# Another order of the same steps in a 16-batch block of attention and experts

## The chip, the cores and the metric

The kernel runs on one core of a Trainium2 chip. A core has five engines that run side by side, each with its own queue of instructions: the matrix engine (TensorE, PE in the profile), VectorE (DVE), ScalarE (ACT), GpSimd (POOL) and SyncE (SP), which here only issues transfers. They tell each other of finished work by semaphores. The metric is the device time of one execution in microseconds; a version's time is the median of its runs.

## What is computed

For 16 batches of 256 rows of 256 numbers the reference computes three things one after the other. First a block with attention, whose layer norms are shifted and scaled by a condition vector:

```python
ada = t_emb @ w_ada + b_ada
sh_msa, sc_msa, g_msa, sh_mlp, sc_mlp, g_mlp = jnp.split(ada, 6, axis=-1)
xn = layer_norm(logmap0(x))
xm = expmap0(xn * (1 + sc_msa) + sh_msa)
q = _to_heads(plin(xm, w_q, b_q))
attn = jax.nn.softmax(scores, axis=-1)
x = mobius_add(residual, expmap0(attn_t))
...
ff = plin(plin(xm, w_f1, b_f1), w_f2, b_f2)
return mobius_add(residual, expmap0(ff_t))
```

Then, on its result, attention over a window of 64 rows with 16 heads, joined by a gate with attention over 64 latents with 8 heads, and added to x:

```python
local = _local_window_attn(Q, K, V)
rem = jnp.einsum('bhsn,bhnd->bhsd', lp, GV)
out = gl * local + gr * rem
return out @ w_out
```

Last a feed-forward network with four low-rank experts, of which two are weighed in for each row, on a modulated copy of x, and added to x again:

```python
base = jnp.einsum('bsd,fd->bsf', x, Wi)
h = jax.nn.relu(base[:, :, None, :] + lora)
out = jnp.einsum('bse,bsed->bsd', w, expert_out)
```

## The kernel before

Everything of a batch stays on the chip between its stages; the 16 batches go through 19 stages, and several batches are under way at once, in different stages. Each engine has for each stage a small generator function (`norm(b)`, `qkv(b)`, `att(b)`, ...), which issues the engine's instructions for that stage and batch and pauses at each `yield`. The function `in_order` steps these generators by a table `ORDER`: for each engine a long string of letters, each of which lets the stage with that letter run to its next `yield`; when a batch's generator is finished, the letter's next appearance begins the next batch. So the table alone decides in which order an engine takes up its work. What may run when is guarded by semaphore waits inside the stages. They stand with the work and move with it, so any table that builds gives the same numbers.

The letters:

```python
STAGES = {"ada": "A", "late": "*", "load": "x", "stat": "s", "prep": "P", "norm": "n", "qkv": "q", "heads": "h",
          "att": "a", "outp": "o", "fin": "f", "norm2": "N", "ff": "F", "fin2": "g", "proj": "p", "maxi": "m",
          "loc": "k", "mix": "w", "moe": "e"}
```

What the later steps need of the stages:

- `ada`: the condition vector times `w_ada`. The matrix engine makes the three rows for batch 0 (groups into `psq` with ST and R) and then those of all 16 batches (the same, 32 wide, on a quarter of the array's columns). VectorE adds the bias: three operations into `bcA` for batch 0, two into `adaR` (TU in the rows) for all. SyncE writes the latter to a table in memory, `ada_rows`, from which later batches read theirs.
- `stat`, `prep`: VectorE makes mean and variance of each row of x with BN_STATS and BN_AGGR, waiting for that batch's transfer of x; `prep` then works out the factors `rln` and `nmr` in some 40 small operations on tiles named `lp`, one depending on the other. A unit of `prep` takes batch 0 alone, then two batches at a time. A step on the tile `mv` of batch b waits for that of b-1.
- `norm`, `qkv`, `heads`: ScalarE normalises (`M` from X, nmr, rln), GpSimd multiplies and adds the modulation of `bcA`, the matrix engine transposes M (L458, `psg<-ident,M`), multiplies with `wqkv`, and VectorE and ScalarE turn the result into heads, which are transposed again (`psg<-ident,U`).
- `att`: four rounds a batch of scores (`psq<-ST`, four at a time in 32 rows of the array each), one exponential over all four banks on ScalarE (`PQ<-psq`), and values (`pso<-PQ,Vg`, in 32 columns each), whose result OT is transposed for `outp`. The scores and the exponential use the same four banks `psq`, so the next scores wait for the exponential before.
- `late`: what is prepared once and is not needed at the very start. On the matrix engine this is above all the product of two weights (`psq<-QK`, half 0 in groups of 512 columns and half 1 in groups of 384), in steps of two matmuls; it uses the banks of `ada` and waits at its start for the last of the three `bcA`.
- `loc`, `mix`, `moe`: window attention (`psq<-QK` in 32 rows, values `pso<-PQ,Vg` and `pso<-PQ,GV`), the gate and out projection, the experts (`psg<-WoT,R`, `psg<-zT,WiT`).

Every matmul on f32 numbers is two passes of the array in the profile; transposes and bf16 matmuls are one. The array is used in several tilings: whole (128 rows by 128 columns), in four row groups (32*128: scores), in four column groups (128*32: values), and smaller ones for masks and the window. The rows print it ahead of the shape. SyncE issues at the start the loads of x of batch 0, `w_ada`, `wqkv`, x of batch 1, weights, x of batch 2, `w_o`, x of batch 3, in this order.

All matmuls are recorded at line 455 and transposes at 458; on VectorE L983, L986 and L989 are the helpers for element-wise operations, L1076 BN_STATS and L1079 BN_AGGR; ScalarE's activation is L1450, GpSimd's modulation L1797. The program on the matrix engine has 13168 passes.

Of the kernel before, what the change touches and what calls it, by code (L numbers as in the profile page):

```python
# [21 lines left out]
def _beta(a, b):  # L22
# [22 lines left out]
    "DVE": [
        "*ssssPPPPPPPPPPPPPPPPPPPPPPPPPPPPPPPPPPPPPPPPPPPAssssnnnnnnnAAssssPPsPsPsPqPsqPsPsPsPqqqPssPsPsqPsqPsqPs",
        "qPsqPsqPqPqPqPqPhhhhPPPP*P*P*P*PPPPPPPPPPPPPPs*Ps*P*P*s*Ps*nP*nP*nP*nP*nP*o*onPonPooqoqoPoPoPoPoPqoqoqoP",
        "oPoPoqPnqPnqPnqPnqPnqPnqPnqPqPqPhhhhooPPPPPPPPffPqfPqfPfPfPfffffffqfqfqfffffqfnqfnqfnqfnqnqnqnqfqfqfhfff",
        "PPPPPhPhPhPPPqPPoPoPoPoPoPPoPoPoPqPoPoPoPoPoPqPoPqPoPoqPoPPPPPPPqPqPqPqPqqqqqqoohNNNfNfNhNfhNfhfofofofoF",
        "fFfFfoFfnFfnFoFnoFnoFnoFfnFfnFfoFfoFfoFfofofofofofqggfgfgfgfgfgfggggogogggggfgfgqggfgfgfgfqgfqgfqfofofof",  # L50
        "qpfqfofqfofqfqfqfsfqfofqfoqsoqohhhhpfpfofofsfofmPoPsoPoPoPoPPPPPmPPPPPPPoPoPPPmPfmPfPfPfPfPfPfPfPfPfPfPf",
        "PfPPfPfPfPfPfPfPfPffffffffffNNNNnNnNnNnnnnFFFFFqFqFFFFFFqFqFqFqoqoqoqoqqnqnqgqgqnhhhhgnognognognogogogog",
        "ogogogooogqNgNgNgNgNgNgwNgwgwgwgwgwgwwoopwfwffsfsfsfsffffffffffffffffffwffpfpfffPPPPPPPPPPPPPPPmePqePePe",
        "PePePqePqmePqePePePePemePqmeFePqePqePqePqePqePqeFePFPqFPqFPqFPhFPFPFPFPFFFFeFhhhengngengngngngngggggggeg",
        "gggNgNgNgNgNgNgNgggeeFFFFoFoFoFoFoFowFowFowpwFowFowFwowFoososswsowogoggggggggggggwgpgpNoNoNgNgNgNgNgffqg",
        "fgfgfgmfqfgfgfqmfqfFfFmfqfmfqfqfFfqfFfqfFqfFqfFqfpqFnqFfqfhfFnfFnfFnfFnsFnsFnsshhhggqggegegegegqegegegeg",
        "egqegegegegegegegegeoeoeoegoeoegogwowogwowowogwowowoooowweoofpfpffffffffffffmwfeffffffffmfefqffmfeffPPPP",
        "PPPmPPPPPPPPPPPPPPPPeeqPPPPPPqPqPqPqPqPqpqPqPqPqPhPsPsPsPsPhhhnnnnnnnNNNNNNNqFFoFoFoFoFoFFFoFoFoFoFoFoFo",
        "eoeoeoeoeoqggwqwgegegegqwgewgewgewgwgwgoNgoNgeNwNgwNgNfNgfgefgefgefgpgfpgfegfefefewgfegmfeFfeFfeFfmfqfFf",
        "FmfqfefqfqmfqfeqfqfqfqfefqFfqFnhFnFnFneFnFnFnFFgggggggggggeeggggghhhpgggggggogooosssoosgogooooooooooooff",  # L60
        "qfffffffffffffwfwffefefwfewfewfewfewewefefwfwfqfefePePeqpPepPePePePePePePePePePPPPPqPPPPPwPPPPPmPqPPPPPP",
        "qmPqPePqPqmPqPePqmPqPqeqqhneNnNnNnNnNnNnNeehhhFFoFoFoFoFoFFFoFoFoFoFoFoFoqoposossogosggggggggggggggggoog",
        "NgNgNgNgNfNfNgfgfffffgwfwfgfwfewfewfefefefFfefefefFwfewfewfeFeFeFweFwfqfeFfefFefqfeFweFeFeFeFpeFpFgggqgg",
        "megggggmeggqggmqeqnqmqeqngqngqngqngqngqnghhhhggggggeeoooooooopooooosossosooooffwfwffefefwfewfewfewfewfew",
        "feeewewfefefqfefefefefefefepfepefefffffPPPPPPPPPPPPPwPPPPmqPPPPPPqPmePPqPPmePPPPmPPqPePqPqPqPqPqPqPqPqqq",
        "heNNNNNnNnNnnnnneehhhFFoFoFoFoFoFFFoFoFoFoFoFoFoqoqogqpogqqogogggqgqgqgqgqgqgqgqNqNqNhNgNgNgNgoogggggwfw",
        "fwfewfewfegfewfewfewfegfefefefegwfwfegfefefenfefnefnefnefnefneneeffffpfpfwmeFmememFeFFFFFFFFFFFFFggggggg",
        "ggggeeggghhhpgogogogoggggggoogogooooooooooqooffffffqffffffqwfwfewfewfewfefefefwfewfewfefeeeeqfwfwfeqfefe",
        "fpepeqeqeqePqePqePqPqPqPqPqwhPmPPPPPPPPPPPmePPpmePPPPPPmPePPPPPPPPPPePPPPPeeNNNNNNNhhhnnnnnnnFFoFoFoFoFo",
        "FFFoFoFoFoFoFoFooooooggqggoogggNgNgNwNwNfNfNgfwfgwfgwfgwfgwfgwfgfgfgfgefgegegefqefgefgefefeqwefweqefgefg",  # L70
        "efefefeepepefwefefefffpmmqqmeqqqmqqeqqqqheeeehhhoooooooooooooooooFooeefefeFefFefFwefwefFefFefFefwefwefwe",
        "fwefwewefFefFefFefFefFwefwefFfFfFfpfpfgfffffPgPmwPePgPgPgPgPgPgPmPePgPgPmPePgPgPgPmPgPgePgPgPgPgPgPgPgPg",
        "PgPPPPgPgPPPPPPPPeeNNNNNNNpoooooFoooFoFoFoFoFoFoFoFoFoFFFFFggggoogggggffegegfegfegfefefefefgefwNfwNfeNfg",
        "NwNfwNfwNfwfewfewfewfewfegfefgefgegepepfegfegfegfgfgfPwgPgPmFPPFPFPFPFPFPFPFPFPFmeFPFpmeFPFmFPPePgPPPPgP",
        "PgPgPgPgPgPgPgPgPgPgPePgPPPPPgPgPgPgggggggggNNgNNNNNeewwwwweeweweweeeeFeweweFeFeFeFeFeFeFeFepepeFeFewFFF",
        "Fgmegpmeggmegggmgggeggggggggggggggggeewweeeweweweweweweweweeeeeepepeeeeeewmpmememeeeewwwwwwwweeeeeweweee",
        "eeepepeeeeeeeeeemwmememeeeeeeeeeeeeeeeeeeeeeeeeeeewwwwwwwwwweeweeeeeeeeeeeeeeeeeeeeeeeeeeeeeeeee",
    ],
# [1940 lines left out]
```

## Time and profile before

| | |
|---|---|
| median of 3 runs | 1182.61 us |
| lowest and highest | 1180.33 and 1185.35 us |
| span of the profiled execution | 1179.4 us |
| matrix engine busy | 1119.6 us, 95% |
| VectorE busy | 862.7 us, 73% |
| ScalarE busy | 678.5 us, 58% |
| GpSimd busy | 241.2 us, 20% |

The span is that of one execution under the profiler, from the first instruction to the last; it lies 3.2 us below the median of the timed runs. The busy time of an engine is the time in which one of its instructions runs. The end of a matmul is worked out, not observed, so that rows of the matrix engine that follow each other without a gap overlap a little. Of the profile, the share of busy time comes first, then tables of busy time in chosen stretches ("windows"), then the timelines, in which each row is a run of like instructions with the idle time ahead of it and what ended it.

### The profile page before, as it was taken

The page shows a single profiled execution, that of the slowest core. Times are in us where ns is not written, and L with a number is a line of the kernel's source. Part 1 is how long each engine was busy: PE and PEld are TensorE (multiplying, and loading weights), DVE is VectorE, ACT ScalarE, POOL GpSimd, SP SyncE. Part 2 cuts the span into 40 slices and gives each one's busy share as a digit, 9 for nine tenths or more (in the row PEclk, how much of TensorE's full clock was granted, in tenths as well). Part 3 has the DMA queues.
Part 4 walks back from the last instruction along what each step waited for, and adds up shares of the span by engine and source line. Part 5 has one row for each costly group of instructions (what it writes and reads, how often), then busy time and mean ns, then how long its engine had stood idle before and what let it go on. Part 6 is the DMA issues. An engine that isn't in the chain of part 4 may idle for free.

```text
span 1179.4 us, 32772 instructions
## 1 busy us (share of the span) xinstructions
PE 1119.6 (95%) x13168; PEld 804.4 (68%) x13168; DVE 862.7 (73%) x3425; ACT 678.5 (58%) x1415; POOL 241.2 (20%) x336
## 2 busy tenths in 40 slices
PE   6879869999999999999999999999999999999998
PEld 3545545777677677777777677777767777777776
DVE  6899978978878887967767966967477895552433
ACT  1567757567765756577564756567474745434231
POOL 2222022042113230131203221022203221210111
PEclk9989989999999999999999999999999999999999
DMA  9410100001000001010000101000001000000000
GB/s 332 138 59 15 37 16 16 24 24 47 25 16 29 17 14 55 3 43 28 29 16 11 38 2 34 15 20 15 9 13 34 16 17 19 21 2 20 3 19 19
DMA packets 27353, 38.59 MB, mean 33 GB/s; under 512 B 3536, under 2 KB 21328, under 8 KB 27200
## 3 DMA queue, kind: packets, MB, share of 16 engines
q1 hardware_dynamic: 25296, 34.29, 9.0%
q8 instruction: 104, 1.70, 0.6%
q10 hardware_dynamic: 1904, 2.20, 0.6%
q14 instruction: 49, 0.40, 0.1%
HBM read 31.79 MB, written 4.29 MB: 31 GB/s over the span
## 4 chain that ended last, share of the span: by engine, by line
PE 73%; DVE 10%; ACT 8%; issue 4%; POOL 3%; DMA 1%; ACTq 0%; DVEq 0%; POOLq 0%
PE psg L455 44%; PE psq L455 16%; PE pso L455 7%; PE psg L458 6%; ACT PQ L1450 3%; POOL M L1797 2%; DVE nm L992 1%; DMA QK<-in_w 1%; ACT M L1450 1%; ACT JA L1461 1%; DVE JD L1005 1%; ACT QK L1450 1%; DVE U L989 1%; DVE R L989 1%; DVE lp L983 1%
## 5 line engine op out<-in xcount | busy, mean ns | idle before, releaser
L1450 ACT ACTIVATE PQ<-psq 128x2048 f32<-128x2048 f32 x112 | 210.3, 1877 | 60.7 <-PE psq L455 60.1
L1822 POOL TENSOR_TENSOR R<-R,rhoT 128x256 f32<-128x256 f32 x128 | 92.8, 747 | 402.3 <-ACT R L1450 402.3
L455 PE MATMUL psq<-QK 32*128 32x128 f32 (+5 forms) x3360 | 128.6, 304 | 1.7 <-DMA QK<-in_w 1.7
L455 PE MATMUL psg<-zT,WiT 128*128 128x256 f32 x480 | 114.5, 381 | 2.1 <-DVE R L989 1.9
L455 PEld LDWEIGHTS psq<-QK 32*128 32x128 f32 (+2 forms) x3360 | 97.3, 166 | 25.7 <-issue 18.4
L455 PE MATMUL pso<-PQ,Vg 128*32 128x256 f32 (+2 forms) x2048 | 109.6, 345 | 3.9 <-ACT PQ L1450 2.4
L455 PE MATMUL psg<-WoT,R 128*128 128x256 f32 x480 | 108.8, 381 | 0.8 <-DVE R L989 0.8
L992 DVE TENSOR_REDUCE nm<-psq 128x16 f32<-128x2048 f32 (+1 forms) x48 | 92.8, 1932 | 20.8 <-PE psq L455 20.0
L1450 ACT ACTIVATE R<-psg 128x512 f32<-128x512 f32 x60 | 35.8, 596 | 119.6 <-PE psg L455 119.4
L455 PEld LDWEIGHTS psg<-WoT,R 128*128 128x128 f32 x480 | 89.1, 190 | 15.0 <-issue 2.4
L455 PEld LDWEIGHTS psg<-zT,WiT 128*128 128x128 f32 x480 | 86.8, 190 | 15.0 <-DVE R L989 2.9
L455 PE MATMUL psg<-wqkv,M 128*128 128x512 f32 (+1 forms) x256 | 92.9, 496 | 0.1
L455 PEld LDWEIGHTS pso<-PQ,Vg 128*32 128x32 f32 x2048 | 56.1, 110 | 47.2 <-issue 21.3
L455 PE MATMUL psq<-ST 32*128 32x256 f32 x1024 | 74.6, 406 | 11.7 <-ACT PQ L1450 10.4
L1450 ACT ACTIVATE QK<-psg,hsel 128x512 f32<-128x512 f32 (+2 forms) x128 | 66.3, 588 | 23.2 <-PE psg L455 23.0
L455 PE MATMUL psg<-h0T,wat 128*128 128x256 f32 x320 | 77.1, 383 | 0.8 <-ACT h0T L1453 0.8
L455 PEld LDWEIGHTS psq<-ST 32*128 32x128 f32 x1024 | 46.7, 186 | 31.8 <-ACT PQ L1450 17.1
L1797 POOL TENSOR_TENSOR M<-M,bcA 128x256 f32<-128x256 f32 x64 | 45.9, 746 | 100.3 <-ACT M L1450 87.9
L455 PEld LDWEIGHTS psg<-h0T,wat 128*128 128x128 f32 x320 | 58.4, 190 | 11.3 <-issue 2.2
L455 PEld LDWEIGHTS psg<-wqkv,M 128*128 128x128 f32 x256 | 45.8, 191 | 28.9 <-issue 23.5
L1812 POOL TENSOR_TENSOR TU<-TU,bcB 128x256 f32<-128x256 f32 x32 | 24.9, 794 | 181.0 <-ACT JA L1461 181.0
L989 DVE SCALAR_TENSOR_TENSOR R<-psg,R 128x512 f32<-128x512 f32 x60 | 40.9, 682 | 26.8 <-POOL R L1822 17.4
(236 smaller groups left out, 2278.9 us busy)
## 6 DMA issues: line engine op xcount, KB each, us to landing
bcB<-ada_rows SPq DMA_DIRECT2D x16, 384.0 KB, 3.4
bcA<-ada_rows SPq DMA_DIRECT2D x15, 384.0 KB, 3.4
X<-in_x SPq DMA_DIRECT2D x16, 256.0 KB, 3.0
XR<-in_x SPq DMA_DIRECT2D x16, 256.0 KB, 2.7
out<-XR SPq DMA_DIRECT2D x15, 256.0 KB, 2.1
QK<-NMT SPq DMA_DIRECT2D x96, 4.0 KB
WiT<-in_WiT SPq DMA_DIRECT2D x1, 1024.0 KB, 4.9
WoT<-in_WoT SPq DMA_DIRECT2D x1, 1024.0 KB, 7.6
```

Source lines behind the costliest of these rows:

```text
L455: return e.matmul(o, lhsT, rhs, start=start, stop=stop, skip_group_check=True)
L458: return e.transpose(o, i, ident[:, :])
L983: return lambda: e.tensor_scalar(o, i, s1, s2, op0, op1) if op1 else e.tensor_scalar(o, i, s1, None, op0)
L989: return lambda: e.scalar_tensor_tensor(out=o, in0=a, scalar=s, in1=b, op0=op0, op1=op1)
L992: return lambda: e.tensor_reduce(o, i, AX.X, op, negate=negate)
L1005: return e.tensor_tensor_reduce(out=o, in0=a, in1=b, scale=1.0, scalar=0.0, op0=ALU.mult, op1=ALU.add, accum_out=acc)
L1450: return e.activation(o, i, func, **kw)
L1461: return e.activation(o, i, ACT.Square, accum_out=acc)
L1797: e.tensor_tensor(M[:, t, :], M[:, t, :], bcv[:, k, :], op).then_inc(*s.mark(b, f"{step}{t}"))
L1812: e.tensor_tensor(UO[:, t, :], UO[:, t, :], bcv(b)[:, 2, :], ALU.mult).then_inc(*s.mark(b, f"z{t}"))
L1822: e.tensor_tensor(R4, R4, rhoT[:, :], ALU.mult).then_inc(*pool_moe.mark(b, f"r{f}{j}"))
```

## The change

The change replaces the table `ORDER` by another one, for all five engines. Nothing else differs: the functions, the operations with their sizes, and the waits inside the steps are the same, and each letter occurs as often as before.

```diff
 ORDER = {
     "PE": [
-        "A*An*qqqq******hh*a**aa*aaanaaooqqqqnoohhqqaqqaaanaaahaqhooaqqaqaaoaaoaNahooFFhanaaqoaaoaaqqaqoopppppphh",
...
+        "AA***nqqqq*****hh*a***aaaaaaanooqqqqonohqhqaqqaaanaaahaqohoqaqaqaaaoaoaaNhoFhFoanaaqoaoqaaqaaqpoopppppmh",
...
     "DVE": [
-        "*ssssPPPPPPPPPPPPPPPPPPPPPPPPPPPPPPPPPPPPPPPPPPPAssssnnnnnnnAAssssPPsPsPsPqPsqPsPsPsPqqqPssPsPsqPsqPsqPs",
...
```

Of the order on an engine, the number at a row's end says how many like instructions stand in a row. First place: VectorE at the beginning of the program. The operations on `lp` are those of `prep` for batch 0, which end in rln and nmr; `bcA` are the three of `ada`. Before:

```order
L989 SCALAR_TENSOR_TENSOR lp<-lp 128x2 [waits dve_prep] x3
L986 TENSOR_TENSOR rln<-lp 128x2 [waits dve_prep]
L989 SCALAR_TENSOR_TENSOR nmr<-mv,rln 128x2 [waits dve_prep]
L989 SCALAR_TENSOR_TENSOR bcA<-psq,U 128x256 [waits pe_ada,d_bada0]
L989 SCALAR_TENSOR_TENSOR bcA<-psq,U 128x256 x2
L1076 BN_STATS bn<-X 128x6 [waits d_hsel,d_bada12,d_x1,d_bada11,d_bada10]
L1079 BN_AGGR mv<-bn 128x2 [waits dve_stat]
```

After, the same stretch around `bcA`:

```order
L1076 BN_STATS bn<-X 128x6 [waits d_x2]
L989 SCALAR_TENSOR_TENSOR lp<-lp 128x2 [waits dve_prep] x4
L986 TENSOR_TENSOR lp<-lp 128x2 [waits dve_prep]
L989 SCALAR_TENSOR_TENSOR lp<-lp 128x2 [waits dve_prep]
L986 TENSOR_TENSOR lp<-lp 128x2 [waits dve_prep] x2
L1079 BN_AGGR mv<-bn 128x2 [waits dve_stat]
L986 TENSOR_TENSOR lp<-lp 128x2 [waits dve_prep]
L986 TENSOR_TENSOR lp<-lp,mv 128x2 [waits dve_prep]
L989 SCALAR_TENSOR_TENSOR bcA<-psq,U 128x256 [waits pe_ada,d_bada0]
L989 SCALAR_TENSOR_TENSOR bcA<-psq,U 128x256 x2
L983 TENSOR_SCALAR lp<-lp 128x2 [waits d_hsel,d_bada12,dve_prep,d_bada11,d_bada10]
```

The statistics of batch 2, with their wait for its x (`d_x2`), now stand ahead of the three `bcA`; those of batch 1 (`[waits d_x1]`) stand another eleven rows higher, and nmr of batch 0 comes nine small operations and one BN_STATS behind `bcA` instead of before it.

Second place: the matrix engine at the beginning, behind the four rows of `ada` for batch 0. Before:

```order
L455 MATMUL psq<-QK 128x512 x2
L455 MATMUL psq<-ST,condT 32x512 x3
L455 MATMUL psq<-R,condT 32x512 x3
L458 MATMUL psg<-ident,M 128x128 x4
L455 MATMUL psq<-QK 128x512 x2
L455 MATMUL psg<-wqkv,M 128x512 x2
...
L455 MATMUL psq<-QK 128x512 x4
L455 MATMUL psq<-QK 128x384 x8
L458 MATMUL psg<-ident,U 128x128 x8
```

After:

```order
L455 MATMUL psq<-ST,condT 32x512 x3
L455 MATMUL psq<-R,condT 32x512 x3
L455 MATMUL psq<-QK 128x512 x6
L458 MATMUL psg<-ident,M 128x128 x4
L455 MATMUL psg<-wqkv,M 128x512 x2
...
L455 MATMUL psq<-QK 128x512 x2
L455 MATMUL psq<-QK 128x384 x8
L458 MATMUL psg<-ident,U 128x128 x8
```

Six matmuls of the weight product (of which the first waits for the last `bcA`) stand together behind the products of `ada` and ahead of batch 0's transposes of M, where two stood before those products and two behind the transposes.

Third place: the matrix engine in the steady part, where batch 2's window attention ends beside scores of a later batch. Before:

```order
L455 MATMUL psq<-QK 128x128 x4
L455 MATMUL pso<-PQ,GV 32x256 x8
L458 MATMUL psg<-ident,OT 128x128 x8
L458 MATMUL psg<-ident,rho 128x128 x2
L455 MATMUL pso<-PQ,Vg 32x192 x4
L455 MATMUL pso<-PQ,Vg 32x128 x4
L455 MATMUL pso<-PQ,Vg 32x192 x4
L455 MATMUL pso<-PQ,Vg 32x128 x4
L458 MATMUL psg<-ident,OTL 128x128 x4
L455 MATMUL psg<-identb,LW 96x128 x4
L458 MATMUL psg<-ident,OT 128x128 x4
L455 MATMUL psq<-ST 128x256 x8
```

After:

```order
L455 MATMUL psq<-QK 128x128 x4
L458 MATMUL psg<-ident,OT 128x128 x4
L458 MATMUL psg<-ident,rho 128x128 x2
L455 MATMUL pso<-PQ,GV 32x256 x8
L455 MATMUL psq<-ST 128x256 x8
L455 MATMUL pso<-PQ,Vg 32x192 x4
L455 MATMUL pso<-PQ,Vg 32x128 x4
L455 MATMUL pso<-PQ,Vg 32x192 x4
L455 MATMUL pso<-PQ,Vg 32x128 x4
L455 MATMUL psg<-identb,LW 96x128 x4
L458 MATMUL psg<-ident,OTL 128x128 x4
L458 MATMUL psg<-ident,OT 128x128 x8
```

The values of the latents (GV) and the scores (ST) have moved between the transposes and the windows' values (Vg), and the transposes of OTL and OT now follow each other.

## Rows read from the trace of the kernel before

**Rows 1.** Busy time of each engine, its share of the span, and instructions.
```profile
span 1179.4 us, 32772 instructions
PE 1119.6 (95%) x13168; PEld 804.4 (68%) x13168; DVE 862.7 (73%) x3425; ACT 678.5 (58%) x1415; POOL 241.2 (20%) x336
```

**Rows 2.** Windows: length, then the columns that the first line names.
```profile
core 0: us, PE busy (x) PEld busy (x) DVE busy (x) ACT busy (x) POOL busy (x), PEclk, DMA share, GB/s
20.00:160.00 140.00, 119.14 (x1040) 72.67 (x1038) 126.27 (x563) 90.21 (x192) 27.18 (x35) 0.95 0.24 78
53.00:160.00 107.00, 89.21 (x826) 56.51 (x826) 97.32 (x433) 72.29 (x160) 18.29 (x26) 0.94 0.11 38
60.00:70.00 10.00, 6.06 (x19) 4.79 (x20) 9.60 (x44) 3.42 (x9) 2.78 (x4) 0.58 0.28 93
200.00:400.00 200.00, 198.12 (x2426) 141.56 (x2419) 164.50 (x653) 130.41 (x275) 41.08 (x54) 1.00 0.08 25
400.00:1080.00 680.00, 671.29 (x8372) 496.83 (x8370) 490.52 (x1896) 395.46 (x826) 136.66 (x190) 1.00 0.07 20
```

**Rows 3.** VectorE's timeline: start, duration, what it is, idle time before it.
```profile
13.10 0.16 DVE L986 TENSOR_TENSOR rln<-lp 128x2 f32<-128x2 f32 x1
13.29 0.16 DVE L989 SCALAR_TENSOR_TENSOR nmr<-mv,rln 128x2 f32<-128x2 f32 x1
14.23 1.09 DVE L989 SCALAR_TENSOR_TENSOR bcA<-psq,U 128x256 f32<-128x256 f32 x3 [0.78 <-PE psq L455]
...
20.93 0.86 DVE L989 SCALAR_TENSOR_TENSOR TU<-psq,hsel,U 96x256 f32<-96x256 f32 x2
22.08 0.43 DVE L1076 BATCH_NORM_STATS2 bn<-X 128x6 f32<-128x256 f32 x1 [0.29 <-DMA X<-in_x]
```

**Rows 4.** The matrix engine's timeline in the first 160 us.
```profile
8.81 2.04 PE L455 MATMUL psq<-ST,condT 128*128 128x512 f32 x2 [8.81 <-DMA R<-in_w_ada]
...
19.55 0.65 PE L458 MATMUL psg<-ident,M 128*128 128x128 f32 x4
...
21.76 5.32 PE L455 MATMUL psg<-wqkv,M 128*128 128x512 f32 x16
26.92 8.76 PE L455 MATMUL psq<-QK 128*128 128x512 f32 x24
35.51 0.60 PE L458 MATMUL psg<-ident,U 128*128 128x128 f32 x4
...
38.77 1.15 PE L455 MATMUL psq<-ST 32*128 32x256 f32 x16
...
53.23 1.06 PE L458 MATMUL psg<-ident,OT 128*128 128x128 f32 x8 [0.81 <-ACT OT L1453]
...
63.16 1.09 PE L458 MATMUL psg<-ident,M 128*128 128x128 f32 x4 [3.71 <-POOL M L1797]
...
159.92 1.46 PE L455 MATMUL psq<-ST 32*128 32x256 f32 x16
```

**Rows 5.** ScalarE's timeline, normalised rows and first exponential of batch 0.
```profile
13.49 1.09 ACT L1450 ACTIVATE M<-X,nmr,rln 128x256 f32<-128x256 f32 x2 [5.28 <-DVE nmr L989]
...
39.99 1.88 ACT L1450 ACTIVATE PQ<-psq 128x2048 f32<-128x2048 f32 x1 [0.29 <-PE psq L455]
```

**Rows 6.** GpSimd's timeline, modulation of batch 0.
```profile
15.39 2.77 POOL L1797 TENSOR_TENSOR M<-M,bcA 128x256 f32<-128x256 f32 x4 [5.49 <-DVE bcA L989]
```

**Rows 7.** The matrix engine's timeline in a steady stretch, with changes of the tiling.
```profile
508.98 1.89 PE L455 MATMUL psg<-WoT,R 128*128 128x256 f32 x8
510.80 1.93 PE L455 MATMUL pso<-PQ,Vg 128*32 128x256 f32 x32
512.67 1.77 PE L455 MATMUL psg<-WG,mT 128*128 128x512 f32 x4
514.27 0.60 PE L458 MATMUL psg<-ident,U 128*128 128x128 f32 x4
514.71 1.67 PE L455 MATMUL psg<-WG,mT 128*128 128x512 f32 x4
```

More of the change, by code:

```diff
@@ new lines @@
+        "omohmaaamaaaNaFnFqqqqakoonkkkkhqhwkawowwopwppawpwpepemqeNmqamqFaameFeeaeeaaeekoeeokeeeeeheNkkhnFFkakpwwp",
+        "aawwpwppopowmqqwmNqqemFaFpamaepenaakphkqhoqkkoekakewwwewaaewppopowemeewemqeqmeeeeeepapamapeaakehnkNqFFoq",
+        "oehkkqkakowwowwaawNpppFwmwqeFeemeemeeaneeamaeeeepaaeoekophhkpeokkkoewqkewwwawppqpawqewmqeemaeemeeaeeaaee",
+        "eeeeNamanFFhookpqkphekkkopewoeNkawwFwaaFwpqpwqpaqeweemaeemeemeeaneamaeeeehehkooepkpeokkkopwkewwwawpppaqe",
+        "qmaewewemeqemeqeeaeeeeamaNeeaaFFhknooqkqheqqkkkoeopeNkawppwwawppwaaawepnwemFeFeempeemeeaehamaeeoeeoekqpe",
@@ L47 @@
[L47 to L56, printed above, removed]
@@ new lines @@
+        "ofoFoFofFfFofFoFoFoFfoofFofFfFoFFofnfofnfnfnnfnfnfggfqgfggogogfggfgfgfgqfgfgfgfgfgfgfgfgfgfgfgfgqgfgqfqf",
+        "oofofqoffqpqfqooffqofofqoqoqoqofqfofopfhffoPPooPmPPhPPhPPmPoPPPoPPmPPPPPPPPPfPfPfPfPhPfPfPPPPPfPPfPPfPPf",
+        "PPffsNNffmNNNNfffsNnffnnnFnfFFnffFnfFqqFFFFFfFqFqFqsqFoqFoqoqqpqogfqnqfqooonogqggnoghgnggogngsghnoghogog",
+        "gogongfgfgqgggoogwgwwwwgfgwwwoofwfwffffffffwpffNhmeNqeNeefNfeefemffeqNfeqeNeNfefeeemffqFeeffefmfeefffefq",
+        "FFFefpqPPFFqFPFPPPPFPFPFFPPPPFPPFqPPqFePePPgePPPPPqPPeoqPPPoPogPPgoPPgqggPePgPgPPPPPqgqhsgghgoggNNeehNoN",
@@ new lines @@
+        "ggogNgogggNgosggphNggFFosFowwooFFFFFnpFnFoFwFowwFFFnnwowwgnnownggggwgggooggggmqqggqgNgNwgsNgfNmggqgNgqgg",
+        "mNgpNqqgqqsFqFFsFFfFpqmFFeseFnnqeeeefFnfFqnfqnFqfneenFFeeehfFhfpfehqsfggheosoeeefffgfefefffggegfogggqooe",
+        "fffowwewosowoweefgowwgoogooogwgfgoewggowsqgfffoffofmefgffffpeffgffwfffgfgfffmgfgqfffffqgfegfmffqfffqfqPP",
+        "PPqqPPPPeePPqPqPPPPPPqPPPPPPmPPPPPPPPPPsqPPPPPPqPPPPphhNnNnpNnNNnhnNnnqNFFooFqFhooFeoooFooFFFFoooFoeFoFF",
+        "oFesqogogeqegewswegwgsgwggweogeowggewwggwgfgNegggNNNgefefgfNfeeggNffegNwgggeFwqeefemefFeFfmFFeeqFmfFeeff",
@@ new lines @@
+        "FnnFqFfqqmfeFFFFFggqosfoqqfnfqeqenqhhggofhoooonogofooooooonngfffgohpfsffpospofgfffffffwgwfqgefegfwgwwwfe",
+        "gefffwfwfffwefffefwfffefsfegqfeefegfeffegfPePPPgPPePPePeeqqgPeePPwPemqePPPPPgPPmPPPegpPqmPPsqPPpPePPqPqP",
+        "PPPPPPPgPgqPqqPqgegeeeNqnqhemnNNNgNgNNhFFnnoFFFoFFnFoonFnFFFFFoFoooooohooqsgoogoohwgggggNggwegeNNgeggeoo",
+        "gegggwNweeggwgwgNgegNwNgweggpeFFswweqFfeeFfqeFFfqffefFeFffFeeFpffeFeqFfFweFfeFemfmqeqeqmfqqqqeffqqqfefhf",
+        "fgfgghhmffefgenooponofoooooonnooogoogoogggfffgfgsofgsofwweewnwewnewffwfewfgffefwnfpefeefefeefewfffhgfffe",
@@ new lines @@
+        "fggfefefeeqffqffeemgfeffePPPPePPPPPPgPePPgwPPPPPgPgmqPqPPPPePPsPPPsPPPPqPPmPPPPgePqPPPqggeNqqqNpNgqqsqNq",
+        "qmeehgNNNFnFnnnhFnooFnFonFFoohFooFqFoFooqoFFFFshpgoooooqoqqoogeeNegNNeweegegNfeqfNwgewqwwfwfNwefewfgeegg",
+        "egffgefqfeqegwNeggweggqgeegngffpgeggqfqqppnfqwfeggffggmnnFqFFFfheFFfFFmeFfFfnFFFmFeFfemogffpofnghgeggeoo",
+        "oooohfgggfoognooofofqoggfogogoogfffffffqgfhfffffffffgfewegwwfwweffewgfgewfwfqqwgqgfwegefefgefeeegqeefefe",
+        "ePePPPegePPwgeqmPPePqPPPqPPqPPqmqPePePqPmPqqePPPPPPPPPPPPPPPmPPPPehPPPehNNpnheepohNNNNNoFFoFFoooFFnoonno",
@@ L97 @@
     "SP": [
-        "nwxxwxx*****AAAnNn*nnNnxnmNxnmNewxNnmxNnmexwNnmNexwnmewxNnNmexwnmewNnmNewnmewNmewNmewNmNewmewmewmewee",
+        "xx**AwAx*xnnw*ANnn*nN*nnxmNnmNxexwNnmxenwxNmNnxmewNnmxewNnmewNnxmNewnmNewmnewNmeNwmewNmNewmewmewmewee",
     ],
```

72 lines of the change are left out of this document (29 added, 43 removed).

## The prediction

> **What bounds the kernel now.** I first read the share of busy time: the matrix engine is busy for 1119.6 of the 1179.4 us of the profiled execution, VectorE for 862.7 [rows 1]. An average hides stages, so next come the windows. From 200 to 400 us the matrix engine is busy for 198.12 of 200 us and from 400 to 1080 for 671.29 of 680; VectorE has a fifth or more of that time free [rows 2]. There the matrix engine is the bound: only less matrix work, or less time between two passes, shortens it. From 20 to 160 us it is the other way round: VectorE 126.27 of 140, the matrix engine 119.14. From 53 to 160 VectorE has 97.32 of 107, so it idles only 9.7 us there [rows 2]. In the opening the time is thus set by VectorE and by the chain of batch 0 through all engines, and what is lost there comes back only from VectorE's few idle microseconds or from matrix work that moves elsewhere. The last views are the timelines of the opening, engine by engine, since the change rewrites what each engine does first.
>
> **What a change of the array's tiling costs.** In the steady part, passes of one shape overlap in the records, because their ends are modelled: the row at 514.27 begins 0.17 before the end of the one at 512.67 (512.67+1.77), and that at 514.71 begins 0.16 before its end [rows 7]. Where the array goes from 128*128 to 128*32 or back it is 0.07 (508.98+1.89 against 510.80) and 0.06 (510.80+1.93 against 512.67). A change costs 0.16 less 0.07, about 0.093 us. On the way back into the full array the group itself is longer too: 1.77 for four passes of WG behind a change, 1.67 for the same four behind none (+0.10), and 0.65 for four transposes behind a change against 0.60 at 35.51 (+0.05) [rows 4, 7]. The Trainium skill, "TensorEngine Tiling (Array Packing)", section Key Properties, says that changing the tiling mode drains TensorE; the row's 0.09 us agrees.
>
> I counted the changes in both programs' order on the matrix engine: 615 before, 583 after, 32 fewer. Of the 32, 28 are changes into the full array: 7 into f32 matmuls, 13 into transposes, 8 into bf16 ones. 32 x 0.093 = 3.0; 7 x 0.10 + 13 x 0.05 = 1.4, together 4.4. The bounds are 3.0 (the longer first group is only the model of the record's end) and 5.8 (all 28 at 0.10). The third place of the order shows how it is done: the mask and global-value groups stand together. But the opening was bound by VectorE, and 14 of the 32 lie in the first two tenths of the program. Behind the start of batch 4's scores (159.92 [rows 4]) 25 remain by my count of that part: at the mean of 4.4/32 each that is 3.5.
>
> **What it costs in the opening.** The first place of the order is VectorE's. Before, the constants bcA are made from 14.23 on, ahead of all statistics but batch 0's [rows 3]. After, the statistics of batch 1 (a wait for its x) and of batch 2 (a wait for its x) stand ahead both of the three bcA and of prep's last step nmr. Batch 2's x is not there before 22.08, where the trace shows VectorE waiting for it with 0.29 idle [rows 3]. Its load stands where it stood in SyncE's queue, so it lands no earlier. Everything behind that wait on VectorE now starts at 22.1:
> - batch 2's first BN_STATS to 22.5, ten small operations at 0.2 (13.10 to 13.29 is the pace [rows 3]) and the aggregate's wait to 24.7, then the three bcA 1.09: 25.8, where it was 15.3. That is +10.5.
> - some nine small operations, a BN_STATS and a memset more to nmr: 28.1, where it was 13.45. ScalarE's normalised rows take 0.6 to the first of the two (1.09 for both, [rows 5]), GpSimd's modulation 2.77 [rows 6]: the modulated rows are there at 31.6, where it was 18.2. +13.4.
> - the matrix engine (second place of the order) now does all six matmuls of the first weight product (12 passes of 512) before batch 0's four transposes of M, and they wait for bcA, since they write the same banks. So it stands still from about 17 (its two condition products are done) to 25.8. By the row at 26.92 (8 passes of 512 columns and 16 of 384 in 8.76) a pass of 512 takes 0.438, so 12 take 5.3; at the lower clock level (1.2 of 2.4 GHz) two took 2.04 at 8.81, so 12 would take up to 12 [rows 4]. Behind 8.8 us of nothing I expect a slow start and take 7.5: transposes at 33.3, where they were at 19.55. +13.7, nearly what the modulated rows alone would give.
> - behind the qkv matmuls (5.32) there are 4 passes of 512 and 16 of 384 left, 4 x 0.438 + 16 x 0.328 = 7.0, where there were 8.76 [rows 4]. Batch 0's heads come at about 47.3 instead of 35.51, less a little because VectorE has moved the preparation of batch 1 behind them: I take +11.3. Its first scores: 50, was 38.77. From there to the transposes of OT four rounds of scores and exponentials (1.88 each, [rows 5]) are one chain, 38.77 to 53.23 before; so 64.5.
>
> SyncE's store of the modulation rows waits for adaR (TU in the rows), whose two operations now come near 32 instead of 20.93 [rows 3]; the loads of batch 6's x, of Bc and of wgkv are queued behind it. Their readers stand behind batch 0's heads, so I cost this at nothing; if that cover is gone it is a wait of a load's few us there, inside the range.
>
> The strict order on VectorE is what makes this wait dear. The Trainium skill, "Perfetto Trace Analysis", section Tensor Engine Instruction, says that ScalarE and VectorE take their instructions strictly first in, first out; the trace agrees, in that no later operation stands before the BN_STATS at 22.08. By that rule alone the change loses; by the drain rule above alone it would gain 4.4 and end at 1178.2.
>
> **What of this arrives at the end.** VectorE at 53 is then about 10 us late (11.3 of the chain, less 1.3 that it works ahead in the meantime). It idles 9.7 between 53 and 160. Part of these gaps are waits for the same chain and shift with it, so nothing of them is given back (+10), or all of them are free (+0.3). I take 2 given back, since the longest matrix gap there, 3.71 at 63.16, ends on GpSimd and the chain of batch 1 behind VectorE [rows 4]. At batch 4's scores (before at 159.92) VectorE has, by the durations of the trace laid along both orders, 2.6 us less work ahead of it: some was moved behind. The matrix engine has more left from there: 3.5 less by changes, 5.2 more by work moved behind, +1.7 in all. In the steady part I found no row at which the new order adds or takes a wait of weight; the distance between what makes a tile and what reads it is alike in both. The tail is all but the same.
>
> Sum: +10 - 2 - 2.6 + 1.7 = +7.1 on the span of 1179.4, so 1186.5. The median of the runs, 1182.6, is 3.2 above that span: 1189.7. **I forecast 1190.**
>
> **The rivals.**
> *The opening absorbs the lag.* If all of VectorE's 9.7 idle us between 53 and 160 are free, +10 - 9.7 - 2.6 + 1.7 = -0.6: 1182, no change. For it: the work of four batches lies at hand there, and the new order was rewritten for all engines at once. Against it: a share of the gaps is latency of a chain. 1179 to 1186: 0.27.
> *Faster: the fewer changes show in full.* If besides that the waits of the opening fall no later than before (the two x land earlier than their rows say, or batch 0's chain wasn't on the path), the sum is -4.4 and down to -5.8: 1177 to 1179. It decides if the BN_STATS of batch 2 begins before 15, where bcA was ready; the row at 22.08 speaks against it. 0.13, with the lower part of the case before.
> *Slower still: the clock.* Where the matrix engine idles in the opening it comes back at the lower level: from 60 to 70 the granted clock was 0.58, behind the 3.71 us of idle time [rows 2, 4], and passes take twice as long. An idle time of 8.8 and one of some 4 around batch 0's heads cost 3 to 5 us of slow passes each, of which I have counted 2; with nothing absorbed, +10 + 5 - 2.6 + 1.7 = +14: 1197. It decides if the windows from 26 to 60 show under 0.8. 0.12.
> *The change of tiling is worth nothing.* If the 0.09 is filled in by the next weight load, the steady part keeps its 5.2 of work and gains nothing: +7.1 + 3.5, 1193. It lies in the range.
>
> **How the numbers follow.** The forecast's case, 1186 to 1194, has 0.48; the others 0.27, 0.13 and 0.12. The range leaves out the fastest 0.1 and the slowest 0.08: 1178 to 1197. Half a per cent, about what a measurement of this kernel tells from no change, is 5.9 us: 1176.7 to 1188.5. Faster than that: 0.08 (the lower part of the third case). Same: the rest of that case, the absorbed case and a quarter of the forecast's, 0.05 + 0.26 + 0.11 = 0.42. Slower: 0.50.
>
> **What the profile of after would show.** VectorE waits for x ahead of a BN_STATS until 22, and bcA ends near 25.8; batch 0's transposes of M are near 33, its first scores near 50. From 53 to 160 VectorE idles under 9.7. Batch 4's first scores come near 165. Between 400 and 1080 a steady batch takes a few tenths less. The prediction is wrong if bcA ends by 18, if batch 4's scores begin by 160 (absorbed), or if the steady part gains or loses over 5 us, which would be waits that I found alike.

## The result and the profile after

The new table takes 1203.68 us (median, 1201.81 to 1205.97), the old one 1182.59 (1180.33 to 1185.35) on the same chip: ratio 1.0181, 95% interval 1.0157 to 1.0206. It is slower by 21 us. I had forecast slower by 7, with a range that ended at 1197. The profiled execution of the new table has a span of 1201.2, 21.8 more than before; the sums below are made on it.

The page of the profile after; its second line answers to the second of [rows 1]:

```profile
span 1201.2 us, 32763 instructions
PE 1124.9 (94%) x13168; PEld 804.0 (67%) x13168; DVE 858.4 (71%) x3425; ACT 675.8 (56%) x1415; POOL 240.8 (20%) x336
```

No engine has more instructions to run; the matrix engine's busy time is 5 us longer, the others' are a little shorter. Most of the time went into standing. The windows of after, for [rows 2]:

```profile
core 0: us, PE busy (x) PEld busy (x) DVE busy (x) ACT busy (x) POOL busy (x), PEclk, DMA share, GB/s
20.00:160.00 140.00, 114.26 (x844) 66.06 (x844) 125.77 (x551) 88.55 (x183) 29.77 (x37) 0.95 0.24 76
53.00:160.00 107.00, 88.45 (x744) 52.65 (x743) 99.45 (x435) 78.36 (x160) 21.06 (x28) 0.97 0.11 36
...
200.00:400.00 200.00, 191.21 (x2364) 136.76 (x2368) 162.51 (x638) 127.90 (x272) 43.02 (x58) 0.99 0.09 27
400.00:1080.00 680.00, 666.71 (x8289) 490.71 (x8286) 490.16 (x1957) 395.82 (x845) 134.75 (x189) 1.00 0.06 20
```

Two things stand here. In the opening the matrix engine did 844 recorded passes between 20 and 160 instead of 1040. And from 200 on, where it is the bound, it is idle for 8.8 of 200 us instead of 1.9, and for 13.3 of 680 instead of 8.7. The second I had not forecast at all.

The opening in VectorE's timeline of after, for [rows 3]:

```profile
17.48 0.43 DVE L1076 BATCH_NORM_STATS2 bn<-X 128x6 f32<-128x256 f32 x1 [9.25 <-DMA X<-in_x]
...
21.92 0.43 DVE L1076 BATCH_NORM_STATS2 bn<-X 128x6 f32<-128x256 f32 x1 [1.94 <-DMA X<-in_x]
...
24.09 1.09 DVE L989 SCALAR_TENSOR_TENSOR bcA<-psq,U 128x256 f32<-128x256 f32 x3
...
26.99 0.16 DVE L989 SCALAR_TENSOR_TENSOR nmr<-mv,rln 128x2 f32<-128x2 f32 x1
```

and in the matrix engine's, for [rows 4]:

```profile
25.23 7.26 PE L455 MATMUL psq<-QK 128*128 128x512 f32 x12 [6.84 <-DVE bcA L989]
32.32 0.60 PE L458 MATMUL psg<-ident,M 128*128 128x128 f32 x4
...
46.85 0.63 PE L458 MATMUL psg<-ident,U 128*128 128x128 f32 x4 [0.88 <-DVE U L986]
...
50.20 1.15 PE L455 MATMUL psq<-ST 32*128 32x256 f32 x16
...
56.68 1.94 PE L455 MATMUL pso<-PQ,Vg 128*32 128x256 f32 x16 [2.18 <-DVE Vg L986]
...
67.25 1.06 PE L458 MATMUL psg<-ident,OT 128*128 128x128 f32 x8 [0.22 <-ACT OT L1453]
...
170.36 1.15 PE L455 MATMUL psq<-ST 32*128 32x256 f32 x16 [1.39 <-DVE nm L992]
```

VectorE stands for 9.25 us for batch 1's x and 1.94 more for batch 2's, and everything behind it is late. Batch 0's scores begin at 50.20 (38.77 before), batch 4's at 170.36 (159.92 before). So of the 21.8 us 10.4 are lost by the start of batch 4's scores, and 11.4 behind it. The medians of experiment 1 below split the loss the same way: 10.1 (1203.7 less 1193.6) and 11.2.

What the matrix engine waited for between 200 and 1100 us (columns: us in total, times, longest), first before:

```profile
PE psg L455 <- DVE R L989: 2.7, 3, 1.1
...
PE psq L455 <- DVE nm L992: 0.2, 1, 0.2
```

and after:

```profile
PE psq L455 <- DVE nm L992: 4.0, 7, 1.0
PE psg L455 <- DVE R L989: 3.2, 5, 1.1
PE psg L458 <- DVE R L989: 2.2, 3, 0.9
...
PE psq L455 <- DMA QK<-NMT: 1.6, 1, 1.6
```

`nm` is the row maximum of the window's and the latents' scores, which VectorE takes from all four banks `psq`; nothing else can be put into these banks until it has read them. One such place after, batch 7's second and third maxima. The matrix engine:

```profile
638.40 1.21 PE L455 MATMUL psq<-QK 32*64 32x128 f32 x64
...
644.51 0.34 PE L455 MATMUL psq<-maskb,identb 32*32 32x128 bf16 x32 [0.81 <-DVE nm L992]
644.78 1.13 PE L455 MATMUL psq<-QK 32*128 32x64 f32 x32
...
652.05 1.15 PE L455 MATMUL psq<-ST 32*128 32x256 f32 x16 [0.96 <-DVE nm L992]
```

and VectorE:

```profile
642.18 2.27 DVE L992 TENSOR_REDUCE nm<-psq 128x16 f32<-128x2048 f32 x1
644.37 0.94 DVE L992 TENSOR_REDUCE hs<-SQ 128x48 f32<-128x768 f32 x1
...
645.30 0.75 DVE L989 SCALAR_TENSOR_TENSOR U<-psg,smn,bqkv 128x512 f32<-128x512 f32 x1
...
650.78 1.22 DVE L992 TENSOR_REDUCE nm<-psq 128x16 f32<-128x1024 f32 x1
```

The scores are there at 639.6 and 645.9, the reductions begin at 642.2 and 650.8. VectorE isn't idle in between: it works through rows that the new table puts ahead. The matrix engine has other work for 4.2 and 5.2 us, and then stands for 0.81 and 0.96. There are many such places and none is large: behind the start of batch 4's scores I count 126 steps of the matrix engine before and 176 after that begin only when somebody else's result is there, with 35.0 and 45.7 us lost, counted from start to start. The number of places depends on how they are counted. The profile's own idle time, which counts from the modelled end of the pass before and leaves out gaps under 0.15 us, gives 38 places with 23.9 us before and 53 with 31.6 after. Both say that the time is in many small waits.

The granted clock doesn't explain it: behind that point it is at its lower level from 160.6 to 167.4 before, and from 172.3 to 179.2 and 203.0 to 206.5 after. Against the usual distance of the same pairs of passes, the matrix engine lost 4.4 us in these stretches before and 4.2 after.

### The profile page after: what moved, and what is told of

Same layout as the page of the kernel before. It is cut to its first block, busy times and chain, and to the rows that moved or that the text cites. A ratio compares the mean times of both kernels' runs of the same rounds, so it can differ in the third digit from the quotient of the medians.

```text
span 1201.2 us, 32763 instructions
## 1 busy us (share of the span) xinstructions
PE 1124.9 (94%) x13168; PEld 804.0 (67%) x13168; DVE 858.4 (71%) x3425; ACT 675.8 (56%) x1415; POOL 240.8 (20%) x336
## 4 chain that ended last, share of the span: by engine, by line
PE 49%; DVE 18%; ACT 5%; issue 4%; POOL 3%; DMA 0%; SPq 0%; DVEq 0%; POOLq 0%; ACTq 0%
PE psg L455 29%; PE psq L455 10%; PE pso L455 5%; PE psg L458 5%; DVE nm L992 3%; POOL M L1797 1%; ACT PQ L1450 1%; DVE R L989 1%; DVE lp L989 1%; DVE X L989 1%; ACT QK L1450 1%; DVE TU L989 1%; DVE lp L986 1%; DVE sf L989 1%; DVE JD L1005 1%
## 5 line engine op out<-in xcount | busy, mean ns | idle before, releaser
L455 PEld LDWEIGHTS psg<-zT,WiT 128*128 128x128 f32 x480 | 86.7, 190 | 15.2 <-DVE R L989 3.5
L455 PEld LDWEIGHTS psq<-ST 32*128 32x128 f32 x1024 | 47.5, 189 | 32.5 <-ACT PQ L1450 15.7
L1797 POOL TENSOR_TENSOR M<-M,bcB 128x256 f32<-128x256 f32 x64 | 47.0, 756 | 89.1 <-ACT M L1450 70.8
```

The costliest lines, as they stand in the source:

```text
L455: return e.matmul(o, lhsT, rhs, start=start, stop=stop, skip_group_check=True)
L1797: e.tensor_tensor(M[:, t, :], M[:, t, :], bcv[:, k, :], op).then_inc(*s.mark(b, f"{step}{t}"))
```

## The experiments

Two theories to begin with. A: the opening's lag and the later waits are two losses, each made by its own part of the table. B: there is one loss, the lag, and the later waits are its echo. All experiments but three (5, 9 and 10) change only the table. A splice of two tables takes for each engine the letters of one up to what had run at a given moment of its execution, and the letters that are left in the other's order. Times are compared with the old table's on the same chip (1181.8 to 1182.6).

**1. The old table up to 159 us, then the new one.**

> The old table up to the start of batch 4's scores (about 159 us), from there the new table's order for all that is left, on all five engines. Theory A, two separate losses: the opening costs 10 us and the new order behind it 11 more by itself (waits of the matrix engine on VectorE): then this is slow by the second alone, 1193 us. Theory B, one loss: the matrix engine's extra waits behind 170 us are only an echo of the late opening (VectorE never gets its lead back): then this runs without them and shows what the fewer changes of tiling are worth, 1178 to 1182 us.

Measured: 1193.56 us, ratio 1.0091 (1.0065 to 1.0116). The order of the opening is the old one, and the matrix engine's waits behind batch 4's scores are 176 with 44.9 us, as in the new table. Theory A: the rest of the new table costs 11 us by itself.

How far a single profile can be trusted shows here too. Batch 4's scores begin at 162.13, 2.2 us later than in the profile of before, though the order up to there is the same; in experiments 5, 6 and 7 it is 161.9, in experiment 11 164.5. Lags at one point of one profile are thus good to some 2 to 5 us, and the sizes below rest on the medians first.

**2. The new table up to 169 us, then the old one.**

> The new table up to 169 us of its own run (just before batch 4's scores), from there the old table's order. Theory A: the opening's lag alone, 1182.6 + 10.4 = 1193 us, and the matrix engine's waits behind it as few as in the kernel before. Theory B: the echo comes with the lag whatever the table behind it, 1200 us or more.

Measured: 1197.61 us, 1.0125 (1.0099 to 1.0152). The size is missed, the question answered: the lag at batch 4's scores is 14.6 us here, 4.2 more than in the new table, since at the splice work lies in an order that neither table has; behind that point the waits are 123 with 34.0 us, as in the kernel before, and the lag grows by 1.4 more. A late opening makes no echo. Theory B is out.

**3. VectorE's opening mended in the new table.**

```diff
     "DVE": [
-        "ssssPPPPPPPPPPPPPPPPssPPPPPPssPPsPPPPPPPPsPPAPsPPPP*PPPPssPPsPsPssPAPPsAnPPnPnnnnnPPPPPsqqqqsqsqPqqqPqPq",
+        "ssssPPPPPPPPPPPPPPPPPPPPPPPPPPPPPPPPPPPPPPPPPPPAsssssss*ssPPsPsPssPAPPsAnPPnPnnnnnPPPPPsqqqqsqsqPqqqPqPq",
```

> The new table with one change, on VectorE alone: the preparation of batch 0 and the three bcA stand ahead of the statistics of batches 1 and 2, so nothing waits for their x before bcA. The matrix engine keeps six weight matmuls ahead of batch 0's transposes, so these come near 21.5 us instead of 32.3 (19.6 before). If that wait is the cause of the opening's lag, batch 4's scores come 8 to 9 us earlier and the kernel takes 1194 to 1196 us. If the lag comes from the rest of the new opening as well, it stays above 1199.

Measured: 1198.35 us, 1.0131 (1.0105 to 1.0156). It gives back 5.3 of the 10 us and lies between the two expectations. Batch 4's scores begin 5.3 us later than before instead of 10.4. So taking away the waits ahead of bcA gives back half of the opening's loss in the new table, and something else there keeps the other half.

**4. The mirror: VectorE's new start, with that wait, in the old table.**

```diff
     "DVE": [
-        "*ssssPPPPPPPPPPPPPPPPPPPPPPPPPPPPPPPPPPPPPPPPPPPAssssnnnnnnnAAssssPPsPsPsPqPsqPsPsPsPqqqPssPsPsqPsqPsqPs",
+        "*ssssPPPPPPPPPPPPPPPPssPPPPPPssPPsPPPPPPPPsPPAPPPPPPPPPnnnnnnnAAssPPsPsPsPqPsqPsPsPsPqqqPssPsPsqPsqPsqPs",
```

> The old table with VectorE's start from the new one: statistics of batch 1 and 2, with their waits for x, ahead of bcA and of the end of batch 0's preparation; all else old. The mirror of the run before: if the wait is the cause, 1182.6 + 10 = 1192 to 1194 us, with bcA ending near 25 us. If VectorE's idle 9.7 us between 53 and 160 absorb it, 1184 to 1187.

Measured: 1193.04 us, 1.0086 (1.0056 to 1.0116). VectorE's timeline of it:

```profile
17.65 0.43 DVE L1076 BATCH_NORM_STATS2 bn<-X 128x6 f32<-128x256 f32 x1 [9.50 <-DMA X<-in_x]
...
22.16 0.43 DVE L1076 BATCH_NORM_STATS2 bn<-X 128x6 f32<-128x256 f32 x1 [2.02 <-DMA X<-in_x]
```

and the matrix engine's:

```profile
25.47 3.64 PE L455 MATMUL psq<-QK 128*128 128x512 f32 x4 [12.41 <-DVE bcA L989]
```

All else is old. The matrix engine stands for 12.41 us until bcA is made, 10.1 us later than before, and its four weight passes behind that take 3.64 us instead of 1.96, since the granted clock is at its lower level from 15.2 to 28.8. The lag is 11.3 us at batch 0's scores, 10.2 at batch 3's, 11.7 at batch 4's and 11.4 at the end. Nothing of it is absorbed by VectorE's idle time between 53 and 160. VectorE's start with the two waits, 11.5 us of idle time, is thus enough by itself for a loss of the opening's size. That it makes 10.7 us here and that its removal in experiment 3 gave back only 5.3 is no contradiction: by the trace of experiment 12, a second thing in the new table holds batch 0 back once the first is gone.

**5. The price of a change of tiling.** In each of the 48 score steps of the window and the 16 third steps of the maxima:

```diff
-                    for i, j, r, o in tiles():
-                        if v == 1:
-                            m = 128 - 128 * (j % 2)
-                            mm(psq[o, i, 256:512], unit(r), MLT[r, m:m + 256], False, False)
...
-                    for c, kt, o in turns[v]:
+                    for late_part in range(2):
+                        if late_part:
+                            for i, j, r, o in tiles():
...
+                        for c, kt, o in turns[v]:
+                            if (o >= 2 * n) != bool(late_part):
+                                continue
```

> The old table and all its steps, with the passes of three kinds of steps in another order inside the step: in the window's scores and in the third step of the maxima the second half of the 32x32 mask passes now stands behind the first half of the scores instead of ahead of all of them. The same 8488 matmuls, no other wait; 727 changes of the tiling instead of 615. At 0.093 us each: +10.4 us, 1193 us, and the matrix engine's waits on others as before. If a change is filled in by the next weight load it is under +3 us; if entering a tile costs less than entering the full array, between the two.

Measured: 1199.05 us, 1.0146 (1.0126 to 1.0166), 17 us for 112 changes. One window step (batch 6, first) in the matrix engine's timeline before:

```profile
583.74 0.44 PE L455 MATMUL psq<-maskb,identb 32*32 32x384 bf16 x32
584.10 1.17 PE L455 MATMUL psq<-QK 32*128 32x192 f32 x24
585.21 0.33 PE L458 MATMUL psg<-ident,OT 128*128 128x128 f32 x1
```

and with the mask passes split:

```profile
590.67 0.38 PE L455 MATMUL psq<-maskb,identb 32*32 32x384 bf16 x16
590.98 0.93 PE L455 MATMUL psq<-QK 32*128 32x192 f32 x16
591.84 0.28 PE L455 MATMUL psq<-maskb,identb 32*32 32x128 bf16 x16
592.05 0.50 PE L455 MATMUL psq<-QK 32*128 32x128 f32 x8
592.48 0.33 PE L458 MATMUL psg<-ident,OT 128*128 128x128 f32 x1
```

From the first mask pass to the transpose it was 1.47 us (585.21 less 583.74) and is 1.81 (592.48 less 590.67): 0.34 for two changes. The waits on others are no more than before (119 with 31.7 us). A change costs 0.15 to 0.17 us here, more than my 0.09; a part of it may be that groups of four tiles that run side by side are broken up, which this kernel can't tell apart. So changes do cost time, and a table that has fewer of them gains by that.

**6. VectorE's maxima taken at once.** In experiment 1's table 25 letters `m` of VectorE are moved up by 1 to 20 letters, to the moment at which their scores had been there.

> As the run with the old opening and the new rest (1193.6), with only VectorE's table changed: 25 of its reductions of the maxima, which there stand 1 to 20 letters behind the moment at which their scores are there, are moved up to it. If the matrix engine waits because the new VectorE order takes these reductions too late, its waits on them fall from 7.0 us to about 1 and the time to 1187 or 1188. If VectorE is simply short of time there, the rows they now push back are late instead and it stays at 1192 or more.

Measured: 1221.78 us, 1.0344 (1.0323 to 1.0366): 28 us slower than experiment 1. Both branches of the expectation are missed. What VectorE waited for (the first row), and then the matrix engine (the others), from 200 to 1150 us:

```profile
DVE nm L992 <- PE psq L455: 44.7, 38, 4.9
```

```profile
PE psg L455 <- DVE R L989: 11.2, 8, 3.0
PE psg L455 <- DVE LW L986: 5.5, 3, 3.1
PE psg L455 <- DVE TU L989: 3.7, 2, 2.0
```

In experiment 1 VectorE's row reads:

```profile
DVE nm L992 <- PE psq L455: 21.2, 15, 4.6
```

The results now come when they were meant to, at most 3.0 us behind their scores, where it was up to 6.2. But VectorE reaches the reductions before the scores are there and stands, 44.7 us in all; what is queued behind them (R of the experts, the gates LW) is late for the matrix engine, which then makes its scores later still. Part of the 28 us is the clock: five times behind 370 us the granted clock fell to its lower level (0.50), for 17 us in all, where in experiment 1 it stayed at the higher one from 197.5 on; at half speed that is up to 8.5 us. Moving one kind of row to where the old run would have wanted it wasn't a mend here: it moved the shortage, and added to it.

**7. The old queue of transfers.** Experiment 1 with SyncE's letters the old ones to the end.

> As the run with the old opening and the new rest (1193.6), with SyncE's table the old one to the end. In the new one the stores of results, which wait for VectorE, stand ahead of the maxima's transfers and of the loads of the modulation in some batches. If that queue makes the waits of 2.1 us on GpSimd's second modulation and 1.3 us on the maxima's transfer, 1190 to 1191; if not, 1193 to 1194.

Measured: 1191.63 us, 1.0086 (1.0071 to 1.0101). That can't be told from experiment 1 (1.0065 to 1.0116). Behind 160 us the matrix engine waits 1.9 us for GpSimd's M, where it was 1.6, and 0.5 for the maxima's transfer, where it was 1.3. If the transfers' order is worth anything, it is under the noise: 1.9 us by the medians, 0.6 by the ratios.

**8. The old table for the first 53 us only.**

> The old table up to 53 us (the end of batch 0's scores and exponentials), then the new one. If the loss of the opening is all made before 53 us, this is 1203.7 less 13 to 14, some 1190 (the stretch from 53 to 160 saves the 2.6 us of VectorE's work that I counted), and batch 4's scores begin between 157 and 160. If the order between 53 and 160 costs as well, it is 1194 or more.

Measured: 1193.52 us, 1.0098 (1.0082 to 1.0113). Batch 4's scores begin 1.0 us earlier than before, at 158.9. So 10.2 of the 21 us are made in the first 53 us (1203.7 less 1193.5), and none between 53 and 160, since experiment 1, with the old order to 159, takes the same (1193.56); the 11 us that are left are those of experiment 1. The two losses add up.

**9 and 10. VectorE relieved, under both tables.**

```diff
-                full = psq.rearrange("p i (e k n) -> p i e k n", e=2, k=2)
+                full = psq.rearrange("p i (e k n) -> p i e k n", e=2, k=2)[:, :, :, :, ::4]
```

and the same for the third maximum. The reductions then read every fourth score only; the maximum over the others is left out.

> The old table; VectorE's 48 reductions of the maxima read every fourth number only (this part of the computation is left out, so the softmax of the window and the latents is shifted by another maximum). Each should take 0.6 instead of 2.3 us, and the scores' banks come free 1.7 us earlier. Of the 9.4 us that the matrix engine waits for VectorE behind batch 4's scores a part goes: 1176 to 1180 us.

> The same shortened reductions with the old opening and the new rest (1193.6 with full ones). Theory A1, the new rest loses its 11 us because its order leaves VectorE's results too little time before the matrix engine reads them: with 70 us of VectorE's work gone the two light kernels lie within 4 us of each other, and this runs at 1178 to 1183. Theory A2, the loss is in the matrix engine's own passes or in other queues: the distance stays near 11 us, 1188 to 1191.

Measured: 1176.87 us with the old table (0.9955, 0.994 to 0.997) and 1179.15 with the new rest (0.9971, 0.9959 to 0.9983). The reductions of the first, then of the second, by tile (duration ns min/median/max):

```profile
L992 DVE TENSOR_REDUCE nm<-psq x48: 409/690/694, 147.6 to 1098.6; 128x16 f32<-128x512 f32 x32, 128x16 f32<-128x256 f32 x16
```

```profile
L992 DVE TENSOR_REDUCE nm<-psq x48: 414/685/694, 148.7 to 1105.2; 128x16 f32<-128x512 f32 x32, 128x16 f32<-128x256 f32 x16
```

The distance between the tables falls from 11.2 to 2.3 us. The same reductions for both, the same matmuls, the same changes of tiling: only VectorE has 64 us less to do (32 x 1.59 + 16 x 0.80), and its results on the banks come 1.6 us sooner. The new rest gains 14.4 us by it, the old 5.7. That is theory A1: 9 of the 11 us are lost because the new order leaves too little time for VectorE's results. The two things that the edit does, less work for VectorE and banks that come free sooner, are not told apart by it.

**11. The old table to 540 us.**

> The old table up to 540 us, then the new one. In the run with the cut at 159 the lag grew by 0.1 us up to batch 10's scores and by 11 from there to batch 14's. If that is the place, this takes 1192 to 1193 us, as with the cut at 159; if the loss was set up earlier and only shows there, 1183 to 1187.

Measured: 1189.45 us, 1.006 (1.0042 to 1.0078), between the expectations: 6.9 us (5.0 to 9.2) are lost behind 540 and by difference some 4 between 159 and 540. The loss has no single place. The lag at batch 10's scores was small in experiment 1 because these scores stand earlier in the new table, with 18 passes fewer ahead of them; at batch 9's and 11's, which have as many passes ahead as before, it was 5.9 and 6.9.

**12. Both openings mended.** Experiment 3, and on the matrix engine batch 0's transposes ahead of four of the six weight matmuls (its letters begin AA*n**qqqq instead of AA***nqqqq).

> As the run with VectorE's opening mended (1198.4), and on the matrix engine batch 0's transposes of M again ahead of four of the six first weight matmuls, as in the old table. There batch 0's transposes waited for the weights to land and came 4 us late. If that is the rest of the opening's loss, batch 0's scores come at 40 to 42 instead of 47.6 and the time is 1193 to 1195; if VectorE's new order (the preparation of batch 1 mixed into batch 0's heads) keeps them back, the scores come at 45 or later and the time is 1197 to 1198.

Measured: 1198.19 us, 1.0135 (1.0118 to 1.0152), the same as experiment 3: the second branch. VectorE:

```profile
22.31 0.43 DVE L1076 BATCH_NORM_STATS2 bn<-X 128x6 f32<-128x256 f32 x1 [2.28 <-DMA X<-in_x]
...
23.78 0.43 DVE L1076 BATCH_NORM_STATS2 bn<-X 128x6 f32<-128x256 f32 x1 [0.16 <-DMA X<-in_x]
...
30.00 1.12 DVE L989 SCALAR_TENSOR_TENSOR U<-psg,smn,bqkv 128x512 f32<-128x512 f32 x2
...
41.30 0.69 DVE L986 TENSOR_TENSOR U<-U,hf 128x512 f32<-128x512 f32 x1
```

and the matrix engine:

```profile
19.01 0.60 PE L458 MATMUL psg<-ident,M 128*128 128x128 f32 x4
...
21.71 1.96 PE L455 MATMUL psq<-QK 128*128 128x512 f32 x4 [0.38 <-DMA QK<-in_w]
...
30.78 1.52 PE L455 MATMUL psg<-wqkv,M 128*128 128x256 f32 x4 [2.82 <-DVE U L989]
...
42.13 0.63 PE L458 MATMUL psg<-ident,U 128*128 128x128 f32 x4 [1.65 <-DVE U L986]
```

The transposes of M are now on time (19.01), and yet batch 0's heads come at 42.13 (35.51 before): VectorE first waits for the x of batches 2 and 3 and works on their statistics and on batch 1's preparation, so that its first U comes at 30 and the matrix engine stands for it for 2.82 and again for 1.65 us. By this trace the other half of the opening's loss is once more work for later batches ahead of batch 0's on VectorE. No run moves that work away, so this half is read from the trace and not shown by an experiment.

## Why the prediction was right and wrong, step by step

The forecast was +7.1 us on the span, the measured change +21.8. Two terms were too small: the lag at batch 4's scores, forecast 5.4 and measured 10.4, and above all the stretch behind it, forecast +1.7 and measured +11.4. The steps, in the prediction's order:

**What bounds the kernel: right.** Matrix engine behind 200, VectorE and batch 0's chain in the opening. Experiments 4 and 8 show the second, the windows the first.

**The opening's chain: right, to about 1 us a step.** Forecast and measured: bcA done at 25.8 and 25.2, nmr at 28.1 and 27.2, transposes of M at 33.3 and 32.3, batch 0's heads at 47.3 and 46.9, its scores at 50 and 50.2. The cause was right too (experiment 4). I had reasoned from batch 2's x only. Most of VectorE's standing, 9.25 us, was already for batch 1's x, and batch 2's added 1.94; since the second wait ends at 21.92, where I had put it, the times behind it came out right.

One reading in it was wrong: I gave the pair of passes at 8.81, 2.04 us, as made at the lower clock level, and no row shows the clock of that moment (the window from 8 to 14 prints 1.00). The size for the slower passes held all the same: twelve took 7.26 us, at a granted clock of 0.74 between 25.2 and 32.5, against 7.5 in the forecast and 5.3 at the higher level.

**The fixed chain behind the scores: 2.7 us short.** Transposes of OT forecast at 64.5, measured at 67.25. I had taken the 14.5 us of before as given; in the new order the first values wait 2.18 us for VectorE's Vg. The lag behind batch 0's scores and values was thus 14 and not 10 to 11.

**What comes back between 53 and 160: the size nearly right, the base not.** I gave 2 + 2.6 back, the trace shows 3.6 (a lag of 14.0 us at batch 0's last values, of 10.4 at batch 4's scores). In experiment 4, where the order in this stretch is the old one, nothing came back: the gaps of VectorE shift with the late chain. Batch 4's scores were forecast 5.4 late and came 10.4 late, by the term of +10, which should have been 14.

**Work moved behind, +5.2: wrong.** It came from durations laid along the two orders. Behind the start of batch 4's scores the traces have 12105 passes before and 12107 after; there was no such work. No run shows this term; what the runs show in that stretch is the 2.3 us less of the next step and the waits of the step after it.

**Fewer changes, -3.5: right in sign, mis-sized.** With the same pairs of passes priced alike in both traces, the matrix engine's passes behind that point take 2.3 us less for 25 changes, 0.09 each, which is what the first part of my price said; the longer records on entering the full array gave nothing. Experiment 5 gave 0.15 and more inside the score steps. The order of size was right and it wasn't what decided.

**"I found no row at which the new order adds or takes a wait of weight": the step that failed.** It put the waits of the steady part at nothing. That was true of each wait and wrong of the sum: 50 more small ones by my count, 11 us in the matrix engine's late steps and 13 with those inside a step. The prediction had named this as a sign of being wrong: a steady part that loses over 5 us. I had compared, for each result, how much matrix work stands between the step that makes it and the step that reads it. What I had not compared is what stands on VectorE ahead of the instruction in between. A reduction of 2.3 us covered by 4 to 5 us of matrix work is safe only if VectorE takes it up at once; before, it did so (its result was there 2.3 to 2.5 us after the scores in nearly all batches), with the new order it came up to 6.2 us after (experiment 1). Experiments 1, 9 and 10 show it: the loss stays without the late opening, and nearly goes when VectorE's part is made light. Experiment 6 shows that moving the reductions alone doesn't mend it, and experiment 11 that it has no single place.

Sum with the measured terms: +10.4 - 2.3 + 13 = +21, of the span's 21.8.

Among the rivals, the slower one (1197, the clock) had the right side and the wrong mechanism: its sign, windows under 0.8 from 26 to 60, didn't come (0.91), and the clock took its part in the twelve weight passes as the forecast had it. The rival that the opening absorbs the lag (0.27) is refuted by experiment 4. The faster one needed batch 2's BN_STATS before 15; it came at 21.92. That a change of tiling is worth nothing is refuted by experiment 5.

What stays open: how the 11 us divide between VectorE's order and the matrix engine's. No run takes one engine's rest from the new table and the others' from the old. Experiments 9 and 10 don't tell apart less work on VectorE and banks that come free sooner. And 2.3 of the 11 us stay when the reductions are light.

## What to carry to other kernels

An order that is searched for fewer of one cost (here the tiling) spends slack that isn't in that count. Before believing it, look for each result not only at how much work covers it on the reading engine but at what stands ahead of it in the queue of the engine that makes it, and add up the small waits: here they came to 11 us, over four times what the fewer changes saved. And in the opening, look for an instruction that waits for a later batch's data and stands in an engine's queue ahead of the first batch's work; here that cost 11 us (experiment 4).
